# Layer-norm tiles of an attention kernel: nine turned by TensorE, or all sixteen loaded as columns

## The reference

```python
x = x + attention(layernorm(x), ctx, ctx, mask, wq, wk, wv, wo)   # 32 query heads, 8 key heads of 128, rotary
x = x + ffn(layernorm(x), qweight, lut4, bias)                    # weights decoded from 4 bit planes and a table

def layernorm(x):
    return (x - mean(x)) / sqrt(var(x) + 1e-5)
```

## Time and profile before

| | us |
|---|---|
| median of 3 runs | 2337.54 (2337.25 to 2340.97) |
| the profiled execution | 2336.49 |
| its span, first to last instruction | 2334.7 |
| PE busy | 2320.7 (99%) |
| DVE busy | 1703.8 (73%) |
| ACT busy | 1108.0 (47%) |
| POOL busy | 566.1 (24%) |

### The profile page before, as it was taken

The page is one execution under the profiler, slowest core; times in us unless marked ns, Lnnn a source line. Parts: engine busy times, 40 slices in busy tenths (PEclk is TensorE's granted clock), DMA queues, the critical chain, the costliest instruction groups (busy, mean ns, idle before and its releaser), DMA issues.

```text
span 2334.7 us, 35083 instructions
## 1 busy us (share of the span) xinstructions
PE 2320.7 (99%) x11846; PEld 1983.3 (85%) x11846; DVE 1703.8 (73%) x3818; ACT 1108.0 (47%) x2458; POOL 566.1 (24%) x675
## 2 busy tenths in 40 slices
PE   9999999999999999999999999999999999999999
PEld 8999999888888888888888888888888888888887
DVE  8888777677777777777776777677777777777763
ACT  6555544646454646455544445444544444444110
POOL 1000001323322233223222333232223232321321
PEclk9999999999999999999999999999999999999999
DMA  7466559545454544444556643343333333334442
GB/s 268 151 205 210 191 176 313 147 135 137 126 131 118 124 135 122 127 123 135 127 163 199 205 143 109 91 118 101 116 91 113 108 100 109 98 106 163 153 135 81
DMA packets 332898, 332.85 MB, mean 143 GB/s; under 512 B 33456, under 2 KB 268080, under 8 KB 332720
## 3 DMA queue, kind: packets, MB, share of 16 engines
q1 hardware_dynamic: 297296, 314.48, 44.8%
q10 hardware_dynamic: 35424, 16.14, 2.7%
HBM read 186.32 MB, written 71.31 MB: 110 GB/s over the span
## 4 chain that ended last, share of the span: by engine, by line
PE 95%; DMA 2%; DVE 1%; SPq 1%; ACT 0%; issue 0%; POOL 0%; ACTq 0%; DVEq 0%
PE bank L887 29%; PE bank L959 28%; PE bank L846 8%; PE bank L997 7%; PE bank L930 7%; PE bank L903 7%; PE bank L823 7%; DMA small_split<-probs 1%; SPq L666 0%; PE bank L784 0%; PE bank L804 0%; DMA ln_row<-in_L_xattn_wk 0%; DVE residual L1861 0%; DMA small_split<-k_scratch 0%; POOL probs L2001 0%
## 5 line engine op out<-in xcount | busy, mean ns | idle before, releaser
L887 PE MATMUL bank<-acts_split,weights_split 128*128 128x512 f32 (+1 forms) x3192 | 743.0, 382 | 0.0
L959 PE MATMUL bank<-weights_split,small_split 128*128 128x512 f32 x3072 | 739.4, 389 | 3.0 <-DVE small_split L1845 1.7
L959 PEld LDWEIGHTS bank<-weights_split,small_split 128*128 128x128 f32 x3072 | 575.3, 188 | 123.4 <-DVE small_split L1845 2.9
L887 PEld LDWEIGHTS bank<-acts_split,weights_split 128*128 128x128 f32 x3192 | 576.5, 188 | 109.6
L2001 POOL TENSOR_SCALAR probs<-probs,row_numbers 128x256 f32<-128x256 f32 x512 | 355.6, 706 | 1196.7 <-DVE row_numbers L1831 1196.7
L1297 ACT ACTIVATE probs<-bank,row_numbers 128x256 f32<-128x256 f32 x512 | 237.4, 470 | 129.4 <-DVE row_numbers L1826 129.4
L1835 DVE STREAM_TRANSPOSE probs<-probs 128x512 f32<-128x512 f32 x250 | 177.6, 710 | 142.3 <-POOL probs L2001 142.3
L1993 POOL TENSOR_TENSOR rope_x<-rope_x,sin_t 128x512 f32<-128x512 f32 (+1 forms) x133 | 166.8, 1254 | 396.3 <-ACT rope_x L1270 396.3
L1840 DVE TENSOR_TENSOR small_split<-small_split 128x512 fp32r<-128x512 f32 x250 | 178.6, 714 | 94.5 <-ACT small_split L1310 94.4
L1820 DVE CUSTOM_DVE_ANT_0 bank<-bank,mask_tile 128x256 f32<-128x256 f32 x512 | 207.2, 446 | 49.3 <-PE bank L903 49.0
L903 PEld LDWEIGHTS bank<-small_split 128*128 128x128 f32 x1536 | 217.5, 190 | 21.9 <-DMA small_split<-k_scratch 1.9
(11 more groups left out here) (126 smaller groups left out, 2159.6 us busy)
## 6 DMA issues: line engine op xcount, KB each, us to landing
small_split<-probs SPq DMA_DIRECT2D x754, 64.0 KB, 2.2
raw<-in_L_xattn_wq SPq DMA_DIRECT2D x61, 512.0 KB, 3.7
raw<-in_L_xattn_wo SPq DMA_DIRECT2D x60, 512.0 KB, 3.9
k_scratch<-small_split SPq DMA_DIRECT2D x64, 256.0 KB, 2.4
v_scratch<-small_split SPq DMA_DIRECT2D x32, 512.0 KB, 2.9
acts_split<-x_scratch SPq DMA_DIRECT2D x32, 512.0 KB, 5.7
mask_tile<-in_mask_BxSxS_ff SPq DMA_DIRECT2D x64, 256.0 KB, 2.9
small_split<-k_scratch SPq DMA_DIRECT2D x64, 256.0 KB, 3.0
```

What stands on the lines that cost most here:

```text
L887: last = pe.matmul(query_bank(j)[:, 0:wide], wq_s[:, h, c, a, :], xT[:, c, m, b * S:b * S + wide], start=c == 0 and i == 0, stop=c == C - ...
L959: last = pe.matmul(out_ps[part][:, :], o_s[:, a, u % 2 * S + t * P:u % 2 * S + (t + 1) * P], wo_s[:, h, m, n * BANK:(n + 1) * BANK], start ...
```

## The change

- `PE_TILES`, `turn_row`, `row_norm`, `x_high`, `x_low`, `store_row` and their semaphores go. All 16 tiles take the way by columns.
- `K_ROW` is now batches 2 to 6 (tiles 0, 2, 4, 6, 8) and `V_ROW` batches 2 to 5 (tiles 1, 3, 5, 7): nine tiles in the context phase still.
- In the context phase a tile's columns lie in `raw`, its high halves in `mask_tile` and in a free piece of `small_split`, which are idle then. `columns_high`, `columns_low` and `store_high` work in two halves, in both phases.
- A K tile's statistics are made beside the keys (one g later than before), its columns are loaded behind V0's store, centered and scaled beside V1 and V2, rounded on ACT ahead of the context quarters, and subtracted between the second and third quarter. It is stored at the start of the next batch.
- A V tile's statistics are made beside the values; its factors are stored behind V1's store. Its columns are loaded in the next batch at g = 2, centered, scaled and subtracted at g = 5, 6, 7, and stored by SP at g = 7.
- `load_columns` waits for the previous tile's low part to be stored; `row_mean` for the previous tile's factors.
- The context loads of batches 3 to 6 move from g = 5, 7 to g = 4, 6.

Core of the diff:

```diff
-    K_ROW = {1: 0, 2: 1, 3: 3, 4: 5, 5: 7, 6: 8}
-    V_ROW = {2: 2, 3: 4, 4: 6}
+    K_ROW = {2: 0, 3: 2, 4: 4, 5: 6, 6: 8}
+    V_ROW = {2: 1, 3: 3, 4: 5, 5: 7}
...
+        def high_half(e, j):
+            if e < A_ROWS:
+                return (mask_t[:, :, :].rearrange("p t k -> p (t k)").bitcast(F32R), R[:, 4096:4608])[j]
+            return x_split_all[:, j * BANK:(j + 1) * BANK]
...
             def load_columns(e):
-                sp.wait_ge(row_step, 4 * e + 4)
+                if e >= A_ROWS:
+                    sp.wait_ge(row_step, 4 * e + 4)
+                elif e:
+                    sp.wait_ge(lo_stored, 16 * e)
+                else:
+                    sp.wait_ge(first_stored, 16)
                 sp.dma_start(cols_tile(e), x_columns[e]).then_inc(cols_in, 16)
...
+            def load_factors(e):
+                sp.wait_ge(factors_out, 16 * (e + 1))
+                sp.wait_ge(cols_step, 2 * e)
                 sp.dma_start(factors_t[:, :], fac_scr[e:e + 1].rearrange("a p k -> a (p k)").to_broadcast([P, 2 * P])
...
# SP, per g of a batch
-                        if g == 0 and b - 1 in V_ROW:
-                            store_row(V_ROW[b - 1], 0)
-                        if g == 3 and b - 1 in V_ROW:
-                            store_row(V_ROW[b - 1], 1)
+                        if g == 2 and b - 1 in V_ROW:
+                            load_columns(V_ROW[b - 1])
+                            load_factors(V_ROW[b - 1])
+                        if g == HKV - 1 and b - 1 in V_ROW:
+                            store_high(V_ROW[b - 1])
+                            store_low(V_ROW[b - 1])
+                        if g == HKV - 1 and b in K_ROW:
+                            store_factors(K_ROW[b])
...
# SP, after the keys
                 store_values(V0, 0, 0)
+                if b in K_ROW:
+                    load_columns(K_ROW[b])
+                    load_factors(K_ROW[b])
                 sp.wait_ge(dq_step, b * DQ_STEPS + 1)
                 load_planes(b + 1)
-                if b in K_ROW:
-                    store_row(K_ROW[b], 0)
...
                 store_values(V1, 1, 0)
-                if b in K_ROW:
-                    store_row(K_ROW[b], 1)
+                if b in V_ROW:
+                    store_factors(V_ROW[b])
...
# PE
                 values(0)
-                if b in K_ROW:
-                    turn_row(K_ROW[b])
                 values(1)
                 values(2)
                 values(3)
-                if b in V_ROW:
-                    turn_row(V_ROW[b])
...
# ACT
             def row_mean(e):
                 act.wait_ge(row_in, 16 * (e + 1))
-                if e > PE_TILES:
-                    act.wait_ge(factors_out, 16 * (e - PE_TILES))
+                if e:
+                    act.wait_ge(factors_out, 16 * e)
...
                 values_high(V2)
-                if b in V_ROW:
-                    row_norm(V_ROW[b])
+                if b in K_ROW:
+                    columns_high(K_ROW[b])
                 for j in range(4):
                     next_context_high(j)
...
# DVE, per g
+                    if g == 5 and b - 1 in V_ROW:
+                        columns_center(V_ROW[b - 1])
+                    if g == 6 and b in K_ROW:
                         row_var(K_ROW[b])
+                    if g == 6 and b - 1 in V_ROW:
+                        columns_scale(V_ROW[b - 1])
+                    if g == 7 and b - 1 in V_ROW:
+                        columns_low(V_ROW[b - 1])
+                    if g == 7 and b in K_ROW:
                         row_scale(K_ROW[b])
...
# DVE, after the keys
                 values_low(V1)
                 if b in K_ROW:
-                    x_low(K_ROW[b], 1, x_ps[1])
+                    columns_center(K_ROW[b])
+                if b in V_ROW:
+                    row_var(V_ROW[b])
                 for k in range(end - 1, end + 1):
                     decode(b, k)
-                if b in V_ROW:
-                    row_var(V_ROW[b])
+                if b in K_ROW:
+                    columns_scale(K_ROW[b])
                 if b in V_ROW:
                     row_scale(V_ROW[b])
                 values_low(V2)
                 for j in range(4):
                     context_low(4 * (b + 1), j)
+                    if j == 1 and b in K_ROW:
+                        columns_low(K_ROW[b])
                 values_low(V3)
```

More of the change, by code:

```diff
@@ L473, in store_high @@
             def store_high(e):
-                sp.wait_ge(cols_hi, e - PE_TILES + 1)
-                sp.dma_start(column_parts(e)[HI], raw.rearrange("p (c n) -> p c n", c=C)).then_inc(hi_stored, 16)
+                sp.wait_ge(cols_hi, e + 1)
+                for j in range(2):
+                    sp.dma_start(column_parts(e)[HI][:, 4 * j:4 * j + 4], high_half(e, j).bitcast(F32)
+                                 .rearrange("p (c n) -> p c n", c=C // 2)).then_inc(hi_stored, 16)
             def store_low(e):
-                sp.wait_ge(cols_lo, e - PE_TILES + 1)
+                sp.wait_ge(cols_lo, e + 1)
                 sp.dma_start(column_parts(e)[LO], cols_tile(e)).then_inc(lo_stored, 16)
[L483 to L490, removed]
             def load_turned(hf, j, c):
@@ L720, in _ @@
                         if j == 0:
[L721 removed]
+                            sp.wait_ge(lo_stored, 16 * NT)
                     for c in {1: (0, 1), 3: (2, 3), 5: (4, 5), 7: (6, 7)}.get(k, ()):
@@ L777, in _ @@
                 pe.transpose(x_ps[1][:, 0:P], ident[:, :], ident[:, :])
-            def turn_row(e):
-                pe.wait_ge(row_ok, e + 1)
-                pe.wait_ge(x_lo, 2 * e)
-                for c in range(C):
-                    last = pe.transpose(x_ps[c // 4][:, (c % 4) * P:(c % 4 + 1) * P],
-                                        ln_row[:, c * P:(c + 1) * P], ident[:, :])
-                    if c % 4 == 3:
-                        last.then_inc(x_tr, 1)
             def turn_rows(f):
@@ L1065, in row_root @@
                 act.activation(x_sd, x_ve, ACT.Sqrt).then_inc(row_sd, 1)
-            def row_norm(e):
-                act.wait_ge(row_r, e + 1)
-                act.activation(ln_row[:, :], ln_row[:, :], ACT.Identity, scale=x_r).then_inc(row_ok, 1)
             def columns_high(e):
-                act.wait_ge(cols_step, 2 * (e - PE_TILES) + 2)
-                act.activation(x_split_all, ln_row[:, :], ACT.Copy).then_inc(cols_hi, 1)
-            def x_high(e, j, src):
-                act.wait_ge(x_tr, 2 * e + j + 1)
-                act.wait_ge(x_stored, 2 * 16 * (2 * e + j))
-                if e == 0 and j == 0:
-                    act.wait_ge(first_stored, 16)
-                act.activation(x_split[:, HI, :], src[:, :], ACT.Copy).then_inc(x_hi, 1)
+                act.wait_ge(cols_step, 2 * e + 2)
+                if e and e <= A_ROWS:
+                    act.wait_ge(hi_stored, 32 * e)
+                for j in range(2):
+                    done = act.activation(high_half(e, j), cols_half(e, j), ACT.Copy)
+                done.then_inc(cols_hi, 1)
             def row_std(f):
@@ L1508, in row_write @@
                 else:
-                    dve.wait_ge(lo_stored, 16 * (NT - PE_TILES))
+                    dve.wait_ge(lo_stored, 16 * NT)
                 if f < PE_ROWS:
```

98 lines of the change are left out of this document (44 added, 54 removed).

## The result

The changed kernel took 2371.99 us (median of four runs, 2371.03 to 2374.51) against 2337.39 before: a ratio of 1.0149, 95% interval 1.0137 to 1.0161. It is 34.6 us slower. The forecast was 2353, slower, with a range to 2366; the direction came true, the size lies above the range.

What follows compares the result with a forecast made beforehand. The prediction took TensorE, busy 99% at full clock, as the bound: 23.2 us of new waits less 7.8 of turns gave +15.4, from 2336.5 to 2351.9 profiled, 1.0 more for the median: 2353. Range 2343 to 2366 (0.60), 2336 to 2366 with short transfers.

Steps and rivals of the forecast that it cites:

- The bound: Whole kernel: PE, busy 99% at full clock, sets the time; PE work removed is weighed against new PE waits.
- Part 1: Row turns of nine tiles in the context phase removed: 9 x 0.87 = 7.8 us less PE work.
- Part 2: Added DVE work and queue order delay the context at batch bounds: at least 2.3 in batches 3 to 5, 1.1 in batch 2.
- floor 8.0: Least new PE waits from DVE and ACT queues in the context phase: 3 x 2.3 + 1.1 = 8.0 us.
- Part 3: Transfers delay the K tile's center: PE waits 5.6 in batches 3 to 5, 3.8 in batch 6, 2.6 in batch 2.
- the factors' round trip ends at about 42, hidden: K tile's factors, stored and reloaded in 3.9 and 4.1 us, return before the columns land at t = 43.0.
- a wait that was priced at 0.1: ACT's V tile row mean waits for K tile factors' store, delaying the fourth value product: 0.1, at most 1 us.
- The sum: Whole kernel: 3 x 5.6 + 3.8 + 2.6 = 23.2 of new waits, less 7.8: +15.4 us.
- Short transfers: Context phase stores and loads take 3.2 and 4.0, new waits 10.5: 2340.2 us, no difference; chance 0.18.
- The full win: Rival: DVE has unseen room at batch bounds, so the turns' time is simply won: 2329.7 us; chance 0.12.
- Late transfers: Context phase transfers of 7.1 and 6.9 plus a late row chain, center at t = 47.0: 2373 us; beyond 2366 chance 0.1.
- Parts at nothing: Row tile 0, attention phase halves, row-sum waits, the last batch's waits and next batches' starts: no cost put on them.

Runs made afterwards that it cites:

- experiment 1: The kernel before with the 72 transposes of the norm tiles left out, all waits and other work kept (nine tiles wrong): 2333.27 us, ratio 0.9977.
- experiment 4: The changed kernel without column loads and factors' transfers in the context phase, order of PE, ACT and DVE operations kept (nine tiles wrong): 2339.21 us, one run.
- experiment 3: The changed kernel with two pairs of row factors used in turn, so row mean waits for the last factors but one: 2373.1 us, ratio 1.0147.
- Experiment 2: The kernel before with only a delay: 6, 10, 14 and 20 small copies on ACT ahead of the context roundings of batches 2 to 5: 2362.05 us, one run.
- experiment 7: The changed kernel with the K tile's column work moved to the next batch's start and two pairs of row factors in turn: 2350.6 us, ratio 1.0054.
- experiment 10: The changed kernel with K tiles' column work in the next batch, two factor pairs, SP transfers reordered, center and scale on POOL: 2381.06 us, ratio 1.018.

## Why the prediction was right or wrong

**The bound** was right: PE, with no room, so that the sign hung on new waits.

**Part 1** (7.8 us for the turns): the profile has no such group any more, and experiment 1 gave 5.6, since one bound then lacked cover. The term was right as work; the 275 ns a piece, weighed in the prediction from "TensorE: Matmul & The Clock Gate" of the Trainium skill (Part 4: PE-mode transpose), would have missed by far more.

**Part 2** (queues, floor 8.0) was right in its mechanism and places, and in its sum by luck: experiment 4 had 7.5 of waits before the keys, at the first and third quarter, but 1.5 in each of the bounds where 2.3 was worked out, and 2.4 before batch 3 for 1.1. In the changed kernel itself the walk can be laid beside the trace: with t counted from 205.46 (208.34, the end of key group 0, less 2.88), DVE's V0 subtraction began at 33.9, for which the text's end at 34.7 gives 34.0; SP's key store went at 31.4, forecast 31.5; the low part at 32.9, forecast 33.0.

**Part 3** had the right mechanism and wrong sizes. Center began at t = 42.0 in batch 2 and at 44.4, 44.9, 45.4 and 45.4 in batches 3 to 6 (t counted in each batch as above); the forecast had 39.9 and 43.0. Both stores ahead of it were sized too short. The low part's, taken at 4.5, took 7.2, 6.7, 5.3 and 7.4 in batches 3 to 6. The factors', taken at 3.9 from a quiet queue, took 6.5, 6.8, 6.3, 5.3 and 6.7 in batches 2 to 6. Landing of all nine factor stores of the phase:

```profile
DMA to landing us min/median/max: 2.8/5.3/6.8
```

The column load took less, 4.1 for 5.5, and gave a part back: in batch 4 the columns were in at t = 43.7. The sentence that "the factors' round trip ends at about 42, hidden" failed in every batch: the factors' load ended last, in batch 4 at t = 44.8.

The late landing also held ACT's row mean, a wait that was priced at 0.1 and "at most 1": it was 2.3, 2.4 and 1.7 before V3 in batches 3 to 5 (in batch 4 row mean at 245.87, behind it the rounding of V1 at 246.93, V3 at 248.28). By experiment 3 this is no cost by itself, since center stands as late either way. Together the new waits were 28.5, forecast 23.2: a fifth too few. By place the agreement is in part luck. In batches 3 to 5 the waits of 5.8, 4.7 and 6.8, forecast 5.7 each, match in sum although center came later, since V3's wait and V3's slower run used up a part of that time. Most of what is missing lies before batch 3 (3.7 for 2.6) and in the last batch (6.7 for 3.8).

**The sum** left a term out altogether, and this is the step that failed most: a wait of PE was priced at its length, with nothing for slower matmuls behind it. Experiment 2 shows that waits of 2.1 to 5.6 bring 1.5 to 2.0 each besides. In the changed kernel longer running came to 13.6, all of what the forecast lacked beside the 5.3 of waits: 15.4 + 5.3 + 13.6 = 34.3. With the waits alone put right the sum gives about 2358, still inside the forecast. No row of the kernel before has the price of a wait, but its clock of 1.00 belongs to a PE that hardly idles, and that number may not be carried to a kernel with gaps. "TensorE: Matmul & The Clock Gate" of the Trainium skill (HAM oscillation — how this bites in real kernels) describes this pattern, a kernel that waits in each tile and starts each one at the lower clock; the runs agree, with 0.57 behind a wait.

**Rivals.** Short transfers (2340) came about only where they were left out, 2339. The full win was never met: 2333 even without any work in the turns' place. Late transfers (2373) has nearly the measured time, for a reason that is only half its own: it had center at t = 47.0 and no slower matmuls.

**Parts at nothing.** The last batch was not clean: its first turn waited 3.3 for the decoding and its products 2.1 for the context (the forecast had 3.8 there in all, as one wait), and its key groups 1.3 for the cosine. The attention phase was as said: 1.0 of the 35.3 lie behind the context phase.

## What to carry to other kernels

Price a new wait of a TensorE that never idled at more than its length, when it is over about 2 us: here the matmuls behind every wait of 3.5 us or more took 1.3 to 2.3 us longer in all, and behind waits of 2.0 to 3.4 most did so too, not all. When a round trip through DRAM stands in an in-order queue, ask what else stands behind it and what is queued in front of its first transfer; moving two loads behind one store, with the factors ahead of another, won back 10 us, more than the change could win in all. And removing one of two waits that hang on the same chain moves the loss, it doesn't lower it.

## What the runs showed of the hardware

- A wait of PE can bring a fall of the granted clock to 0.50, in the wait or up to 1.4 us behind it. In the changed kernel it fell before PE took up work again at 150.08 (columns as in the view by stretches above):

```profile
149.50:150.00 0.50, 0.00 (x0) 0.00 (x0) 0.50 (x2) 0.50 (x2) 0.00 (x0) 0.53 0.43 164
```

  Behind the wait of 3.51 it fell 0.5 us after the keys had begun, behind experiment 2's wait of 2.10 it fell 1.3 us after.
- In the context phase of all runs, all sixteen waits of 3.5 us and more brought the fall. Of sixteen waits of 2.0 to 3.4 that began at full clock ten did and six did not; the shortest that did was 2.10, the longest that did not 3.33, in experiment 7:

```profile
363.68 3.13 PE L866 MATMUL bank<-small_split,weights_split 128*128 128x256 f32 x24 [3.33 <-DVE rope_a L1410]
```

  Outside experiment 10, twelve waits of 1.25 to 1.83 us with no longer one close by brought none (key run 5.99 behind 1.40). In experiment 10 one of 1.73 did, and so did pairs of waits of 1.2 to 1.8 some 3 us apart. The length alone does not decide.
- A store of 1 KB (two numbers of 4 bytes from each of 128 partitions), nine times in the context phase, landed after 5.3 us by the median. Behind a megabyte of other stores, in batches 3 to 6, it took 5.3 to 6.8, longer than the 4.1 of the column loads of 512 KB by the median.
- DVE's context subtraction, with two operands in SBUF, took 692 ns in the kernel before (24 of them, 703 at most). In experiment 10 the median was 693, but those beside POOL's operations, which have two such operands too, took up to 2916. With PSUM as one source DVE's subtraction stayed at 684 (697 at most), also beside POOL (0.68 at 260.58). Here are the groups of experiment 10, 150 to 383 us (busy, mean ns):

```profile
L1434 DVE TENSOR_TENSOR small_split<-residual,small_split 128x512 fp32r<-128x512 f32 x18 | 28.5, 1632 | 1.4 <-ACT small_split L1053 1.3
L1585 DVE TENSOR_TENSOR small_split<-bank,small_split 128x512 fp32r<-128x512 f32 x28 | 19.1, 684 | 17.0 <-ACT small_split L1160 16.9
```

  "SBUF — State Buffer" (Who interferes with whom) of the Trainium skill says that a DVE instruction with two SBUF inputs contends with a GpSimd instruction that reads SBUF; the rows agree (1632 and 684). How much of the 1632 is waiting and how much slower running, no row here tells.
